# Stacking the turned pieces of four tiles by 24 DMAs from one buffer, in a fused layer with differential attention

## The reference

```python
x = x + 0.5 * ffn(layernorm(x))        # 16 experts choose 256 rows each by softmax scores
x = x + attn(layernorm(x))
x = x + 0.5 * ffn(layernorm(x))

def attn(x):                           # S=512, H=16 heads, KVH=4, D=32
    q = rope((x @ Wq).reshape(b, s, H, 2 * D))
    k = rope((x @ Wk).reshape(b, s, KVH, 2 * D))      # repeated for 4 heads
    v = (x @ Wv).reshape(b, s, KVH, D)
    energy = einsum('bqhad,bkhad->bahqk', q, k)       # a = 0, 1: two halves of a head
    scores = softmax(causal(energy) / sqrt(D))
    diff = softmax(causal(scores[:, 0] - lam * scores[:, 1]))
    att = einsum('bhqv,bvhd->bqhd', diff, v)
    return rmsnorm(att).reshape(b, s, E) @ Wo
```

## Time and profile before

| | us |
|---|---|
| median of 3 runs | 1805.55 |
| lowest, highest | 1804.53, 1811.26 |
| the profiled execution | 1807.81 |
| its span, first to last instruction | 1806.0 |

### The profile page before, as it was taken

One profiled execution on the slowest core, in us unless ns is written; L12 is line 12 of the kernel. 1 busy time (PEld: TensorE's weight loads), 2 busy tenths in 40 slices (PEclk: granted clock), 3 DMA queues, 4 the chain that ended last, 5 costly groups with the idle time before them and its releaser, 6 DMA issues. The chain is left out here.

```text
span 1806.0 us, 43973 instructions
## 1 busy us (share of the span) xinstructions
PE 1472.8 (82%) x10688; PEld 1044.2 (58%) x10688; DVE 1440.5 (80%) x5505; ACT 1259.0 (70%) x3426; POOL 1247.3 (69%) x1493
## 2 busy tenths in 40 slices
PE   3997644889889999999998989898989999898610
PEld 3543322667666666666666666666666777676310
DVE  5778525888888989898989898898989877874477
ACT  2353334887788888888888888888889866865320
POOL 4421443786788989898989898888889866665300
PEclk9999776887899999999989999999999866766855
DMA  8013322111111111111111111121211100001186
GB/s 310 1 57 120 122 58 46 30 35 33 34 44 46 47 45 49 50 48 46 49 45 45 45 45 51 45 52 46 53 46 48 43 24 17 22 18 36 42 323 250
DMA packets 178953, 115.99 MB, mean 64 GB/s; under 512 B 139089, under 2 KB 139473, under 8 KB 178898
## 3 DMA queue, kind: packets, MB, share of 16 engines
q1 hardware_dynamic: 178898, 115.34, 21.7%
HBM read 50.26 MB, written 33.55 MB: 46 GB/s over the span
## 5 line engine op out<-in xcount | busy, mean ns | idle before, releaser
L1671 ACT ACTIVATE ex<-bank,nbias 128x512 f32<-128x512 f32 (+3 forms) x1024 | 530.7, 543 | 85.5 <-DVE bank L1214 84.0
L1214 DVE TENSOR_SCALAR_CACHE_REDUCE bank<-bank,nesc 128x512 f32<-128x512 f32 (+3 forms) x1024 | 503.5, 552 | 96.5 <-PE bank L1929 95.4
L1959 PEld LDWEIGHTS bank<-vs,pr 128*128 128x128 f32 x2560 | 358.0, 219 | 14.5 <-issue 11.0
L1959 PE MATMUL bank<-vs,pr 128*128 (+1 forms) x2560 | 359.0, 293 | 6.3 <-issue 5.0
L1515 POOL TENSOR_SCALAR ex<-ex,esum,gam 128x128 f32<-128x128 f32 (+3 forms) x512 | 356.8, 707 | 0.0
L1927 PE MATMUL bank<-ks,hall 96*128 (+2 forms) x1024 | 261.9, 332 | 97.3 <-ACT ex L1671 71.6
L1688 ACT ACTIVATE pr<-bank 128x128 f32<-128x128 f32 (+3 forms) x512 | 231.7, 453 | 91.5 <-PE bank L1941 90.4
L1941 PE MATMUL bank<-cst,df 128*128 128x128 f32 x1280 | 266.3, 312 | 34.9 <-ACT pr L1688 34.9
L1239 DVE CUSTOM_DVE_ANT_0 df<-ex 128x128 f32<-128x128 f32 (+3 forms) x512 | 279.3, 560 | 10.6 <-POOL ex L1515 3.3
L1522 POOL TENSOR_SCALAR df<-df,dmax,rsum 128x128 f32<-128x128 f32 (+1 forms) x256 | 279.7, 1093 | 0.0
L1671 ACT ACTIVATION_READ_ACCUMULATOR ex<-bank,nbias 128x1 f32 x1024 | 225.7, 220 | 0.0
(11 more groups left out here) (358 smaller groups left out, 2935.9 us busy)
## 6 DMA issues: line engine op xcount, KB each, us to landing
hall<-turned SPq DMA_DIRECT2D x360, 64.0 KB, 2.1
x_dram<-hall SPq DMA_DIRECT2D x8, 1024.0 KB, 4.9
hall<-x_dram SPq DMA_DIRECT2D x8, 1024.0 KB, 14.7
c_y<-y_dram SPq DMA_DIRECT2D x8, 1024.0 KB, 14.8
out_dram<-hall SPq DMA_DIRECT2D x8, 1024.0 KB, 4.7
hall<-in_x SPq DMA_DIRECT2D x7, 1024.0 KB, 13.7
x<-x_dram SPq DMA_DIRECT2D x28, 256.0 KB, 2.6
x_dram<-x SPq DMA_DIRECT2D x28, 256.0 KB, 2.1
```

The lines of the kernel that those rows point to most:

```text
L1214: dve.tensor_scalar(part, part, nesc[:, 0:1], None, ALU.mult, ALU.min, accum_out=nbias[:, j, i, a:a + 1]).then_inc(bias_done.sem, 1)
L1671: ac.activation(ex[j % 4][:, a, lo:hi], energy(j, i)[:, a, :], ACT.Exp, bias=nbias[:, j, i, a:a + 1], scale=-1.0, accum_out=esum[:, j, i, ...
L1959: mm = pe.matmul(bank[:, 7, t * DV:(t + 1) * DV], pr[j % 2][:, lo + k * P:lo + (k + 1) * P], val, start=(k == 0), stop=(k == t))
```

## The change

The turned pieces of tiles 0 to 3 go into one buffer, `four`, in which the 128 columns of each tile stand side by side, so that a chunk is a row of 512. It takes the place of x1 of tiles 5 to 14 in `hall`, which have to be in memory by then: ACT waits for `x1_st[1]` to `x1_st[3]` before its first copy. ACT's waits for the stacks are gone. SP loads tile 5 first; then `stack_four` waits for the twelfth turned piece and stacks all four tiles by 12 DMAs into `ks` and 12 into `qs`, each with runs of 512 columns (1 KB) in the place of 128 (256 B). Tile 4 is turned into `turned` and stacked as before, once these have landed, since its place in the second ring overlaps `four`.

```diff
@@ -975,8 +975,11 @@
                      (df[3][:, 0:512], pr[0][:, 0:512], pr[1][:, 0:NK]))
             p_split = (split[:, :, :], ex[2][:, :, :].rearrange("p a n -> p (a n)").bitcast(F16)
                        .rearrange("p (a n) -> p a n", a=2))
-            p_turned = (turned[:, :, :, :], ex[3][:, :, :].rearrange("p a n -> p (a n)").bitcast(F16)
-                        .rearrange("p (a c s) -> p a c s", a=2, c=NC))
+            four = x1_at(AHEAD, NC).rearrange("p t e -> p (t e)").bitcast(F16).rearrange("p (a c s) -> p a c s", a=2, c=NC)
+
+            def p_turned(u):
+                return four[:, :, :, u * P:(u + 1) * P] if u < TB else turned[:, :, :, :]
+
             p_norms = (norms[:, 0:10], norms[:, 10:20])
 
             def p_bank(u, n):
@@ -1101,8 +1104,10 @@
             @blk.sync
             def _(sp):
 
-                for s in (stacked_q, stacked_k, x2_st, y2_st):
+                for s in (x2_st, y2_st):
                     sp.sem_inc(s, 16)
+                for s in (stacked_q, stacked_k):
+                    sp.sem_inc(s, (TB - 1) * 192 + 16)
 
                 def load(u):
                     lo_done.wait(sp, u - 1, apart_s)
@@ -1136,10 +1141,15 @@
                     y_out.wait(sp, u, apart_s)
                     sp.dma_start(flat(y2_t[ds(u, 1), :, :]), yb[:, :]).then_inc(y2_st, 16)
 
-                def stack_first(u):
-                    for done in (stacked_q, stacked_k):
-                        sp.wait_ge(done, u * 192 + 16)
-                    stack(u, None, p_turned[u % 2])
+                def stack_four():
+                    turned_out.wait(sp, TB * 3 - 1)
+                    for dst, order, c0, c1, done in ((ks, (0, 0, 1), CQ, NC, stacked_k),
+                                                     (qs, (0, 1, 0), 0, CQ, stacked_q)):
+                        to = dst[:, :, :].rearrange("p (r c i) n -> p r c i n", r=2, i=4)
+                        for j, part in enumerate(order):
+                            for i in range(4):
+                                sp.dma_start(to[j * D:(j + 1) * D, 0, :, i, :],
+                                             four[i * D:(i + 1) * D, part, c0:c1, :]).then_inc(done, 16)
 
                 sp.sem_inc(x_in, 16 * AHEAD)
                 for g in range(2):
@@ -1147,12 +1157,11 @@
                 load_again(0)
                 for g in range(2, NT // 4):
                     sp.wait_ge(x1_st[g], 16)
-                stack_first(0)
-                stack_first(1)
                 load(AHEAD)
-                stack_first(2)
-                stack_first(3)
-                stack_first(4)
+                stack_four()
+                for s in (stacked_q, stacked_k):
+                    sp.wait_ge(s, TB * 192 + 16)
+                stack(TB, None)
                 with sp.Fori(0, BEHIND) as K:
                     load(K + (AHEAD + 1))
                     stack(K + AHEAD, K)
@@ -1786,10 +1795,11 @@
 
                 def first_chunks(u, n):
                     c0, c1 = CHUNKS[n]
+                    if u == 0 and n == 0:
+                        for g in range(AHEAD // 4, (AHEAD + NC - 1) // 4 + 1):
+                            ac.wait_ge(x1_st[g], 16)
                     rt_done.wait(ac, 3 * u + n)
-                    if u >= 2:
-                        ac.wait_ge(stacked_k if c0 >= CQ else stacked_q, (u - 1) * 192 + 16)
-                    ac.copy(p_turned[u % 2][:, :, c0:c1, :],
+                    ac.copy(p_turned(u)[:, :, c0:c1, :],
                             p_pair(P_C[n])[:, :, 0:(c1 - c0) * P].rearrange("p a (c s) -> p a c s", s=P))\
                       .then_inc(turned_out.sem, 1)
 
```

## The result

| | before | changed |
|---|---|---|
| median of 10 runs, us | 1808.76 | 1794.62 |
| lowest, highest | 1801.68, 1813.89 | 1783.47, 1797.63 |
| the profiled execution | 1807.81 | 1786.06 |
| its span | 1806.0 | 1784.3 |

The ratio is 0.991, with a 95% interval of 0.9884 to 0.9935: faster by 12 to 21 us. The difference of the medians is 14.1 us. The profiled execution of the changed kernel is one of its short ones, so the 21.7 us between the two spans overstates the change; the stretch that was changed has to be read by itself.

A forecast was written before the change was run, and what follows sets the result against it. SP's 96 DMA issues were taken as the bound. First issue at 243.2, ks issues to 251.0, 1.3 to the burst, 14.3 of qs transfers and 0.5 gave 267.1, 17.7 us earlier: 1805.55 - 17.7 = 1788, range 1780 to 1800.

The forecast's parts named there:

- The bound: Before the attention, SP's 96 DMA issues (4 tiles x 24, 0.65 us each) set when PE can start.
- SP's first issue: After tile 3's last turned piece is copied at 243.0, SP issues its first stacking DMA at 243.2.
- The twelve for ks: SP's twelve issues into ks take 7.8 us, ending at 251.0; each 64 KB transfer keeps up.
- The price of a qs transfer: Each 256 KB transfer into qs moves at 220 GB/s: 1.19 us, 14.3 for twelve, setting the end instead of the issues.
- The sum: First energy matmul at 267.1 in place of 284.84, 17.7 us earlier, all of it off the end: median 1788.
- Costed at nothing: ACT's strided copies, its new wait for x1 stores (15 us of cover) and tile 5's earlier load add no time.
- Tile 4's last piece: Tile 4's final turned piece is there by about 251 to 253, beneath the transfers' 267.
- Passing it on: From the attention's start the queues are the same, so the whole 17.7 us comes off the end.
- Rival 1: Longer runs go faster: 0.76 us per qs transfer, start 22.9 us earlier, 1782.6; 22 in 100.
- Rival 2: A burst's mean is the true qs rate: 119 GB/s, start 5.6 us earlier, 1800.0; 8 in 100.
- Rival 3: Attention starts early, but TensorE's clock stays at 0.66 for the second 42 us: 8 us lost, 1795.9; 6 in 100.
- Rival 4: Slower than before: qs transfers at 60 GB/s, 4.4 us each, PE starts 20.4 us late, 1826; 4 in 100.

The follow-up runs named there:

- e3_96_issues: The large buffer alone: ACT waits for no stack, but SP still stacks tile by tile with the 96 DMAs of the kernel before; 1803.4 us, ratio 0.9997 to before.
- e4_all_partitions: Changed kernel with its twelve qs transfers replaced by sixteen of 256 KB, 128 partitions to the same 128, stacking left out; 1788.7 us, one run.
- e2_pairs: Changed kernel, but tiles 0 and 1 stacked by 24 DMAs after tile 1, tiles 2 and 3 by 24 more after tile 3; 1779.8 us, ratio 0.987 to before.
- e1_q_first: Changed kernel, but the twelve qs transfers are issued ahead of the twelve for ks; 1789.8 us, ratio 0.9911 to before.

## Why the prediction was right, point by point

- **The bound.** Right: SP's chain of stacks, and e3_96_issues shows it by taking only ACT's waits away. 63.7 of its 68.0 us are the 96 issues.
- **SP's first issue.** Forecast at 243.2, 54.0 after the start of the stage; it came at 54.15. The chain through POOL's sum, ACT's cast and copy held.
- **The twelve for ks.** 7.8 forecast, 8.28 to the first issue for `qs`: 0.5 late, with the 0.1 above 0.6.
- **The price of a qs transfer.** This is the term that was mis-sized. I took 1.19 us (220 GB/s) from the top of a burst; from the first issue for `qs` to PE it took 81.31 - 62.43 = 18.9 us where 1.3 + 14.3 + 0.5 = 16.1 were forecast. Less the 1.8 at the ends that is 17.1 for twelve, 1.42 each, 184 GB/s. The top of a burst in the earlier trace rows was not a rate that holds: 2.8 us. The two ends were sized well: the first large transfer's bytes begin 1.3 us after its issue, and PE starts some 0.6 after the last packet (267.9), where 0.5 were forecast. The windows' 198 is above the 184 since it leaves out the slower first 3 us (168 GB/s) and the thin last one.
- **The sum.** 17.7 forecast, 14.3 in the profile of the stretch and 14.4 in its repeat; 0.6 and 2.8 are the difference. The measured medians are 14.1 apart. The time of 1788 was forecast against 1805.55; with more runs the kernel before has 1808.76, and the changed one 1794.62, so that 3.2 of the 6.6 us by which the forecast was low are this shift of the base, and 3.4 are the two misses.
- **Costed at nothing.** ACT's copies (863 ns for 866), the new wait for x1 (no such idleness), the load of tile 5 (issued at 231.12, 10 us ahead of the stacks): right. Tile 4's last piece was there 60.7 us after the start of the stage (at 248.00), where 251 to 253 in the trace before are 61.8 to 63.8. PE had done its part at 59.7, 4.1 before the later of these, and the transfers ended 3.4 later than forecast, so its wait was 21.6 us and not 14. That error was hidden beneath the transfers and cost nothing: here the forecast was right without being right about PE.
- **Passing it on.** Right within what can be told: the stretch from the first product to the end scatters by 12 us over twelve profiles, with no relation to when it began.
- **Rival 1** (0.76 us a transfer, some 345 GB/s, 22 in 100) drew a line from the bursts of 32 partitions to the x1 stores of 128, and e4_all_partitions (338) shows where such a rate holds: on 128 partitions. **Rival 2** had a burst's mean, 119 GB/s; the ramps were ramps. **Rival 3** needed the second 42 us of the attention at 0.66. They ran at 0.82 in the changed kernel and in its repeat, against 0.90 before, and PE was busy 37.16 us in them for 36.65: half a microsecond, not 8. Nor does that go with the change: in its second 42 us e3_96_issues, whose attention starts as late as before, had 0.78, and e2_pairs 0.90. **Rival 4** would have needed 98 GB/s.

## What to carry to other kernels

Where a queue issues many small DMAs, count issues before bytes: here each cost 0.65 us of SP for 16 KB as for 64 KB, and the stalls of the engine that fills the buffers were only its echo. Making them fewer and larger pays until the bytes take over, and it also takes overlap away, since nothing can start before the last piece is there; here two batches (e2_pairs) beat one. Price the larger transfer at the rate of its own shape over a sustained stretch, and count its partitions: here a band of 32 or 64 moved at little more than half the rate of 128.

## What the runs showed of the hardware

- Copies inside SBUF of 256 KB with 1 KB runs: 338 GB/s on 128 partitions, 187 on 64, 179 to 198 on 32. With the source's half changing from most transfers to the next 211 over 13 us, and 246 to 295 for 1.5 us of them; with two queues 217 over 10 us.
- Transfers with runs of 512 B on 32 partitions (e2_pairs) kept up with SP's issues at 187 GB/s, with the DMA engines busy at 0.83.
- SP's issues stretched where the transfers were slower than they: twelve took 12.96 us in the place of 7.8, and sixteen took 11.94, 21.26 and 22.49 at 338, 187 and 179 GB/s. Here a stretched issue was a sign of saturated transfers. Issues on ACT's queue took 0.64 us at the shortest and 0.7 to 1.0 in the median, beside SP's, which stretched too.
- The same instructions behind the first energy product took between 1510.6 and 1522.9 us in different executions, and the first stage between 185.7 and 189.4, at mean granted clocks of the whole execution from 0.858 to 0.870. The second 42 us of the attention ran at a granted clock between 0.74 (e1_q_first) and 0.90, wherever they began.
